# Quantizing the feed-forward weights inside the attention loop instead of ahead of it

## The chip, the cores and the metric

The kernel runs on one core of one Trainium2 chip. The time is the device time of one launch in microseconds (us). A core has five engines, each with an instruction queue of its own: TensorE (PE in the profile; PEld are its weight loads), VectorE (DVE), ScalarE (ACT), GpSimd (POOL) and SyncE (SP), which here only issues DMAs. They run side by side and wait for one another through semaphores. Sixteen DMA engines move the data; SP and ACT each issue into a queue of their own, and both queues are served by the same sixteen.

## The reference

```python
x = x + attention(layernorm(x), w_att_val, wv_w, wv_b, out_w, out_b)   # x: 16 x 512 x 256
x = x + ffn(layernorm(x), w_gate, w_up, w_down)                        # 256 -> 704 -> 256

# attention, 16 heads of 16 columns
att = softmax((x_h @ w_att[h]) @ x_h.T / sqrt(16));  o = att @ v_h;  return o @ out_w.T + out_b
# ffn
def fp4_quant_dequant(x):      # blocks of 16 along the last dim
    scale = max(max(abs(block)) / 6, 1e-12)
    return grid_round(abs(block / scale)) * sign * scale        # grid 0 .5 1 1.5 2 3 4 6
def fp4_linear(x, w): return fp4_quant_dequant(x) @ fp4_quant_dequant(w).T
return fp4_linear(silu(fp4_linear(x, w_gate)) * fp4_linear(x, w_up), w_down)
```

The three weight matrices of the feed-forward part are quantized once, before they are used. They do not depend on x. The change is about where this is done.

## The kernel before, in words

Three blocks follow one another, with a barrier of all engines between them.

`first_block` prepares batch 0 and the weights. It normalizes x, transposes it, makes the products q and the values v, and stores x and q, each split in a high and a low part, as rows in DRAM (`x_rows`, `q_rows`; `store`, L228). It also loads all three feed-forward matrices (L233 to L240), quantizes them in four chunks on DVE (`amax`, `scale_of`, `invert`, `in_units`, `shift`), ACT (`magnitude`) and POOL, transposes them on PE (`turn`), and stores them in DRAM (L253 to L256). The block ends when the last of these stores has landed.

`attention_block` runs over 16 batches b, in each over four quads g of four heads, and in each quad over four steps j; below, (g, j) names a step. Batches 1 to 13 run in a loop. While quad i is worked on, the row maxima of quad i+2 are made. In each step PE computes two maximum tiles (L858), the scores of four heads (L866, L869), two more maximum tiles, and then what else the step has: the product of probabilities and values (L885), or one or two of the small tasks that `IN_STEP` lists for the step. DVE reduces each of the four maximum tiles to one column (`reduce_max`, L1086), ACT makes the exponentials (L995), POOL splits and adds. All tiles of PSUM that are not scores share a ring of four banks, in the order of `TILES_IN_RING`. A tile may be written when the tile four places before it in the ring has been read. Two empty places (None) fill the ring's list up to 88.

The order on each engine is written out by hand, in the functions `quad` and `batch` of each engine. All waits stand in that order: an engine that waits for a semaphore holds back everything behind it.

SP's part of a batch, in order: for each quad g it stores half of the next batch's rows if g is even (`store_half`), waits until the scores of quad g are done, waits until the stores have landed (`stored`), and loads the stacks x_stack and q_stack of the next batch for this quad (`load_stacks`, L803 and L807, six DMAs).

ACT also issues DMAs: it stores the transposed maxima to DRAM (`store_maxima`, L1044), loads them as a stack (`load_maxima`, L1054), and loads x two batches ahead (L1058). PE's scores of a quad wait for the loaded maxima.

`ffn_block` then works through 64 tiles of 128 rows. It finds the weights in SBUF: SP loads them during the last batch.

Of the kernel before, what the change touches and what calls it, by code (L numbers as in the profile page):

```python
# [4 lines left out]
F32 = mybir.dt.float32  # L5
# [5 lines left out]
P = 128  # L11
B, T, E = 16, 512, 256
H, D = 16, 16
I = 704
# [11 lines left out]
STORES = (4 + 2) * 16  # L26
FK = [(k * P, min(P, I - k * P)) for k in range((I + P - 1) // P)]
# [41 lines left out]
def build(nc, x, w_att, wv_w, wv_b, out_w, out_b, w_gate, w_up, w_down, out):  # L69
# [8 lines left out]
    gate_up_kept = dram("gate_up_kept", [P, HALVES, 2 * I], F32)  # L78
    down_kept = dram("down_kept", [P, len(FK), E], F32)

    whole = ExitStack()
    with whole:
        def sb(name, shape, dt=F32, ctx=whole):
# [19 lines left out]
                 "stored0", "stored1")}  # L103

        with ExitStack() as prep:
            tiles = dict(
                qw_high=sb("qw_high", [P, HALVES, P], F32R, prep),
                qw_low=sb("qw_low", [P, HALVES, P], F32R, prep),
                vw_high=sb("vw_high", [P, HALVES, E], F32R, prep),
                vw_low=sb("vw_low", [P, HALVES, E], F32R, prep),  # L110
                v_bias=sb("v_bias", [P, E], F32, prep),
                xn=xn, splits=splits, v_dense=v_dense, stats=stats, mean_var=mean_var, rstd=rstd,
                minus_half=minus_half, eps=eps, ident=ident, x_all=x_all, out_T=out_T, out_bias=out_bias,
                x_rows=x_rows, q_rows=q_rows, gate_up_kept=gate_up_kept, down_kept=down_kept, sems=sems,
            )
            with ExitStack() as ctx:
                first_block(nc, ctx, x, w_att, wv_w, wv_b, out_w, out_b, w_gate, w_up, w_down, **tiles)
            with ExitStack() as ctx:
                attention_block(nc, ctx, x, max_rows, **tiles)
# [16 lines left out]
def first_block(nc, ctx, x, w_att, wv_w, wv_b, out_w, out_b, w_gate, w_up, w_down,  # L136
                xn, splits, v_dense, stats, mean_var, rstd, minus_half, eps, ident, x_all, out_T, out_bias,
                x_rows, q_rows, gate_up_kept, down_kept, sems, qw_high, qw_low, vw_high, vw_low, v_bias):
# [6 lines left out]
    def sem(name):  # L145
        return ctx.enter_context(nc.semaphore(name))

    NGU = 2 * I // P
    SPLIT, REST = I // P, I % P
    FULL = I // P  # L150
    gu = sb("gu", [P, NGU, E])
    gu_units = sb("gu_units", [P, NGU, E])
    gu_mag = sb("gu_mag", [P, NGU, E])
    dn = sb("dn", [P, HALVES, I])
    dn_units = sb("dn_units", [P, HALVES, I])
    dn_mag = sb("dn_mag", [P, HALVES, I])
    scale = sb("scale", [P, (NGU * E + HALVES * I) // BLK])
    inverse = sb("inverse", [P, (NGU * E + HALVES * I) // BLK])
    gate_up_T = sb("gate_up_T", [P, HALVES, 2 * I])
    down_T = sb("down_T", [P, len(FK), E])  # L160
# [15 lines left out]
    x_first, gu_loaded, dn_loaded, vw_loaded, ow_loaded, qw_loaded, bias_loaded, kept = (  # L176
        sem(n) for n in ("x_first", "gu_loaded", "dn_loaded", "vw_loaded", "ow_loaded", "qw_loaded",
                         "bias_loaded", "kept"))
# [6 lines left out]
    dn_quantized = sem("dn_quantized")  # L185

    amax_done, scale_done, inverse_done, units_done, mag_done, shifted, unshifted, quantized = (
        sem(n) for n in ("amax_done", "scale_done", "inverse_done", "units_done", "mag_done", "shifted",
                         "unshifted", "quantized"))


    def chunk(tiles, at, width, first):
        flat = [t[:, :, :].rearrange("p r e -> p (r e)")[:, at:at + width] for t in tiles]
        k = slice((first + at) // BLK, (first + at + width) // BLK)
        return (*flat, scale[:, k], inverse[:, k])

    GU_CHUNKS = [(r, min(4, NGU - r)) for r in range(0, NGU, 4)]
    CHUNKS = [chunk((gu, gu_units, gu_mag), r * E, n * E, 0) for r, n in GU_CHUNKS]
    CHUNKS.append(chunk((dn, dn_units, dn_mag), 0, HALVES * I, NGU * E))

# [4 lines left out]
    GATE_UP_FROM = len(TURNS)  # L207
    for c, (r, n) in enumerate(GU_CHUNKS):
        for a in range(HALVES):
            TURNS.append(([gu[:, k, a * P:(a + 1) * P] for k in range(r, r + n)],  # L210
                          gate_up_T[:, a, r * P:(r + n) * P], (quantized, c + 1)))
    for n in range(HALVES):
        TURNS.append(([dn[:, n, at:at + w] for at, w in FK[0:4]], down_T[:, 0:4, n * P:(n + 1) * P],
                      (dn_quantized, 1)))
    for k, (at, w) in enumerate(FK[4:]):
        TURNS.append(([dn[:, n, at:at + w] for n in range(HALVES)], down_T[0:w, 4 + k, :],
                      (dn_quantized, 1)))

    with nc.Block() as block:
        @block.sync  # L220
        def _(sp):
# [4 lines left out]
            def store(a, dst, rows):  # L226
# [4 lines left out]
            load_x(0, 2, x_first)  # L231
            sp.dma_start(vw[:, :, :], wv_w.rearrange("(n p) e -> p n e", p=P)).then_inc(vw_loaded, 16)
            sp.dma_start(gu[:, 0:SPLIT, :], w_gate[0:SPLIT * P, :].rearrange("(r p) e -> p r e", p=P))\  # L233
              .then_inc(gu_loaded, 16)
            sp.dma_start(gu[0:REST, SPLIT, :], w_gate[SPLIT * P:I, :]).then_inc(gu_loaded, 16)
            sp.dma_start(gu[REST:P, SPLIT, :], w_up[0:P - REST, :]).then_inc(gu_loaded, 16)
            sp.dma_start(gu[:, SPLIT + 1:NGU, :], w_up[P - REST:I, :].rearrange("(r p) e -> p r e", p=P))\
              .then_inc(gu_loaded, 16)
            sp.dma_start(v_bias[:, :], wv_b.partition_broadcast(P)).then_inc(bias_loaded, 16)
            sp.dma_start(dn[:, :, :], w_down.rearrange("(n p) k -> p n k", p=P)).then_inc(dn_loaded, 16)  # L240
# [9 lines left out]
            for c, (r, n) in enumerate(GU_CHUNKS):  # L250
                sp.wait_ge(moved, GATE_UP_FROM + HALVES * (c + 1))
                cols = slice(r * P, (r + n) * P)
                sp.dma_start(gate_up_kept[:, :, cols], gate_up_T[:, :, cols]).then_inc(kept, 16)  # L253
            sp.wait_ge(moved, len(TURNS))
            sp.dma_start(down_kept[:, 0:FULL, :], down_T[:, 0:FULL, :]).then_inc(kept, 16)
            sp.dma_start(down_kept[0:I - FULL * P, FULL, :], down_T[0:I - FULL * P, FULL, :]).then_inc(kept, 16)  # L256
            sp.wait_ge(bias_loaded, 32)
            for a in range(HALVES):
                sp.wait_ge(stored[a], STORES)
            sp.wait_ge(kept, 16 * (len(GU_CHUNKS) + 2))  # L260

        @block.gpsimd
        def _(pool):
# [20 lines left out]
            for c, (src, units, mag, sc, inv) in enumerate(CHUNKS[:-1]):  # L284

                pool.wait_ge(unshifted, c + 1)
                pool.tensor_tensor(blocks(src), blocks(units), spread(sc, BLK), ALU.mult).then_inc(quantized, 1)

        @block.scalar
        def _(act):  # L290
# [12 lines left out]
            def magnitude(c):  # L303
                act.wait_ge(units_done, c + 1)
                act.activation(CHUNKS[c][2], CHUNKS[c][1], ACT.Abs, scale=2.0 ** 22).then_inc(mag_done, 1)


# [8 lines left out]
            magnitude(0)  # L316
# [3 lines left out]
            magnitude(1)  # L320
            move(1)
            magnitude(2)
            for n in range(2, 2 + HALVES):
                move(n)
            magnitude(3)
            for n in range(2 + HALVES, len(TURNS)):
                move(n)
# [1151 lines left out]
```

## Time and profile before

| | us |
|---|---|
| median of 3 runs | 1574.35 (1573.51 to 1575.29) |
| the profiled execution | 1576.56 |
| its span | 1574.5 |
| `first_block` and its barrier end | 55.0 |
| first scores of batch 0 | 86.0 |
| `ffn_block` begins, about | 1003 |

Rows of the page and of the trace read as follows. A timeline row is start, duration of the whole group, engine, line, operation, destination and sources, shapes and number of instructions; in brackets stands how long the engine was idle before, and what ended this. A row of windows gives the stretch, its length, then the busy time and the instructions of PE, PEld, DVE, ACT and POOL, TensorE's granted clock as a share of full speed, the busy share of the DMA engines and the GB/s. SPq and ACTq are DMAs issued by SP and ACT; their duration is the time that issuing takes.

### The profile page before, as it was taken

Reading aid. Unit: us, or ns where it says so; the run is one execution under the profiler, and the core shown is the slowest. Engines: PE = TensorE matmul, PEld = TensorE weight load, DVE = VectorE, ACT = ScalarE, POOL = GpSimd, SP = SyncE. Lnnn points to the kernel's source line nnn. Section 1 sums busy time; section 2 is a strip of 40 time slices with the busy share of each in tenths; the row PEclk is TensorE's granted clock in tenths of the full one; section 3 lists DMA queues with packets and bytes.
Section 4 is the critical chain, followed back from the end, with each engine's and each line's share of the span. In section 5 each row is a group of like instructions: output and inputs, shape, how many; then the busy total and the mean of one; then the engine's idle time right before and its main releaser. Section 6 shows DMA issues by size and latency. Waiting matters only on the chain. (4 is left out here: it accounts for less than half of the span.)

```text
span 1574.5 us, 33229 instructions
## 1 busy us (share of the span) xinstructions
PE 1460.8 (93%) x8874; PEld 910.1 (58%) x8874; DVE 1313.4 (83%) x2603; ACT 864.9 (55%) x1778; POOL 634.1 (40%) x868
## 2 busy tenths in 40 slices
PE   3389999999999999999999998699999999999998
PEld 3145555555555555555555554466666666676665
DVE  7588887888888888788788774499999999999995
ACT  2157777677677677777767767233333333333332
POOL 2135445345345444544544521133434334343341
PEclk8589999999999999999999999799999999999999
DMA  5534564555554455455455460000000000000000
GB/s 195 149 111 136 140 160 124 148 149 133 138 159 124 127 160 148 122 136 162 122 142 156 112 163 29 1 10 14 17 17 13 17 13 17 17 13 17 13 17 20
DMA packets 81762, 144.07 MB, mean 91 GB/s; under 512 B 19904, under 2 KB 39488, under 8 KB 81600
## 3 DMA queue, kind: packets, MB, share of 16 engines
q1 hardware_dynamic: 64992, 134.19, 30.7%
q10 hardware_dynamic: 16736, 9.46, 2.7%
q8 instruction: 17, 0.28, 0.1%
q14 instruction: 17, 0.14, 0.0%
HBM read 81.67 MB, written 61.93 MB: 91 GB/s over the span
## 5 line engine op out<-in xcount | busy, mean ns | idle before, releaser
L1086 DVE TENSOR_REDUCE neg_max<-ring 128x1 f32<-128x512 f32 x1024 | 636.7, 683 | 137.6 <-PE ring L858 136.5
L995 ACT ACTIVATE probs<-scores 128x512 f32<-128x512 f32 x1024 | 528.9, 605 | 211.6 <-PE scores L869 206.0
L1411 PE MATMUL gu_bank<-splits,f_x_T 128*128 128x352 f32 x1024 | 317.3, 463 | 2.1 <-ACT f_x_T L1389 2.1
L858 PE MATMUL ring<-x_stack,q_stack 64*128 64x512 f32 x1024 | 234.5, 455 | 45.5 <-DVE neg_max L1086 16.8
L1411 PEld LDWEIGHTS gu_bank<-splits,f_x_T 128*128 128x128 f32 x1024 | 191.5, 192 | 99.3 <-issue 3.0
L885 PE MATMUL ring<-probs,v_quad 128*32 128x512 f32 x2048 | 246.2, 598 | 1.9
L858 PEld LDWEIGHTS ring<-x_stack,q_stack 64*128 64x128 f32 x1024 | 99.1, 188 | 196.2 <-DVE neg_max L1086 132.6
L866 PE MATMUL scores<-q_stack,x_stack 64*128 64x512 f32 x1024 | 206.0, 396 | 2.1 <-ACT probs L995 2.1
L869 PE MATMUL scores<-max_stack,max_ones 64*128 64x512 f32 x1024 | 203.8, 392 | 0.0
L1239 POOL TENSOR_TENSOR f_rstd<-f_mean_var,eps 128x1 f32<-128x1 f32 x64 | 44.7, 699 | 330.9 <-DVE f_mean_var L1349 330.9
L733 POOL TENSOR_TENSOR pv_rows<-pv_more,pv_rows 128x512 f32<-128x512 f32 x64 | 82.2, 1285 | 199.7 <-ACT pv_more L1001 194.9
L1369 ACT ACTIVATE h_T<-h_bank 128x512 f32<-128x512 f32 (+1 forms) x128 | 49.0, 435 | 195.0 <-PE h_bank L1421 195.0
L1429 PE MATMUL y_bank<-splits,h_T 128*128 128x256 f32 x640 | 150.4, 382 | 1.1 <-ACT h_T L1369 1.1
L885 PEld LDWEIGHTS ring<-probs,v_quad 128*32 128x32 f32 x2048 | 53.6, 109 | 126.3 <-issue 74.2
L1429 PEld LDWEIGHTS y_bank<-splits,h_T 128*128 128x128 f32 x640 | 117.5, 192 | 15.4 <-issue 0.8
L710 POOL TENSOR_TENSOR max_cols<-neg_max,one 128x16 fp32r<-128x16 f32 x64 | 13.8, 216 | 244.2 <-DVE neg_max L1086 244.2
L869 PEld LDWEIGHTS scores<-max_stack,max_ones 64*128 64x128 f32 x1024 | 98.1, 185 | 20.0
L866 PEld LDWEIGHTS scores<-q_stack,x_stack 64*128 64x128 f32 x1024 | 98.2, 186 | 19.9 <-ACT probs L995 8.3
L1249 POOL TENSOR_TENSOR hq<-h_level,h_scale 128x704 f32<-128x704 f32 x64 | 88.5, 1383 | 25.2 <-DVE h_level L1294 25.2
L1306 DVE TENSOR_SCALAR f_xn<-x_all,f_mean_var,f_rstd 128x256 f32 (+1 forms) x64 | 83.2, 1300 | 10.0 <-POOL f_rstd L1242 5.8
L1389 ACT ACTIVATE f_x_T<-x_bank 128x256 f32<-128x256 f32 x64 | 24.6, 384 | 119.3 <-PE x_bank L1399 119.3
L1381 ACT ACTIVATE gate<-gu_bank 128x352 f32<-128x352 f32 x128 | 58.7, 458 | 40.1 <-PE gu_bank L1411 40.0
(130 smaller groups left out, 2076.8 us busy)
## 6 DMA issues: line engine op xcount, KB each, us to landing
x_rows<-splits SPq DMA_DIRECT2D x128, 256.0 KB, 2.8
x_stack<-x_rows SPq DMA_DIRECT2D x128, 256.0 KB, 4.3
q_stack<-q_rows SPq DMA_DIRECT2D x256, 128.0 KB, 4.3
q_rows<-splits SPq DMA_DIRECT2D x64, 256.0 KB, 2.2
out_dram<-x_all SPq DMA_DIRECT2D x64, 128.0 KB, 1.7
x_all<-in_L_attn_x_dram ACTq DMA_DIRECT2D x14, 512.0 KB, 6.4
max_stack<-max_rows ACTq DMA_DIRECT2D x128, 8.0 KB
splits<-gate_up_kept SPq DMA_DIRECT2D x1, 1408.0 KB, 7.5
```

What stands on the lines that cost most here:

```text
L733: pool.tensor_tensor(pv_rows[g % 2][:, :], pv_more[:, :], pv_rows[g % 2][:, :], ALU.add)\
L858: pe.matmul(bank(tiles[m])[:, :], row_tile(q_stack[q], m)[:, p, s * P:(s + 1) * P], row_tile(x_stack[q], m)[:, p, :], start=True, stop=Tru ...
L866: pe.matmul(scores[ROWS * p + m][:, :], row_tile(x_stack[g], m)[:, p, j * P:(j + 1) * P], row_tile(q_stack[g], m)[:, p, :], start=True, st ...
L869: pe.matmul(scores[ROWS * p + m][:, :], row_tile(max_ones, m)[:, 0, :], row_tile(max_stack[g % 2], m)[:, p, :], start=False, stop=True).th ...
L885: m = pe.matmul(bank(tile)[VW * h:VW * h + VW, :], v[q][:, j, h, :], probs[j][:, k, :], start=(j == steps[0]), stop=(j == steps[1]))
L995: act.activation(probs[j][:, k, :], scores[k][:, :], ACT.Exp).then_inc(p_ready, 1)
L1086: dve.tensor_reduce(neg_max[g % 2][:, at:at + 1], tile[:, :], AX.X, ALU.max, negate=True).then_inc(m_used, 1)
L1249: pool.tensor_tensor(blocks(out), blocks(level), spread(scale, BLK), ALU.mult).then_inc(done, 1)
L1306: dve.tensor_scalar(xn[w][:, :], x_all[:, bass.ds(m, 1), :].rearrange("p o e -> p (o e)"), mean_var[w][:, 0:1], rstd[w][:, :], ALU.subtrac ...
L1381: act.activation(gate[1 - u][:, k, :], gu_bank[k][:, :], ACT.Silu).then_inc(gate_done, 1)
L1411: m = pe.matmul(gu_bank[c][:, :], x_T[u][:, a, :], gate_up_T[:, a, c * CH:(c + 1) * CH], start=(a == 0), stop=(a == HALVES - 1))
L1429: m = pe.matmul(y_bank[:, :], h_T[u][0:width, k, :], down_T[k][0:width, :], start=(k == 0), stop=(k == len(FK) - 1))
```

## The change

Nothing of the feed-forward weights is left in `first_block`. It loads x of batch 0 alone first and x of batch 1 a little later, and at its end SP loads the stacks of quads 0 and 1 of batch 0.

At the start of `attention_block` ACT issues twelve DMAs (`copy_weights`) that copy the three matrices from DRAM to DRAM into 42 slabs of 128x128 (64 KB each). Each of batches 0 to 13 takes three slabs. SP loads them into `w_raw` (`load_weights`), DVE, POOL and ACT quantize them in steps (1, 0) to (2, 2), and in step (1, 1) of the following batch PE turns them, ACT copies them to `w_turned` and SP stores them (`store_weights`). Two more things change in the steps: the ring gets the tile "weights" in (1, 1) and one empty place fewer, and in (3, 3) "proj1" now comes before "rows2". POOL's two instructions "tie" and "units" take the place of DVE's one instruction `in_units`.

```diff
-    IN_STEP = {... (1, 1): ("rows0",), ... (3, 3): ("rows2", "proj1")}
+    IN_STEP = {... (1, 1): ("weights", "rows0"), ... (3, 3): ("proj1", "rows2")}
+    WEIGHTS = {(1, 0): "peak", (1, 1): "scale", (1, 2): "invert", (2, 0): "shift", (2, 1): "unshift"}
     POOL_STEP = {...
-                 (2, 1): ("halves",), (2, 2): ("deviation",), ...
+                 (1, 2): ("tie", "units"), ...
+                 (2, 1): ("halves",), (2, 2): ("deviation", "quantized"), ...
# SP, batch(b), in each quad g
                         sp.wait_ge(s_ready, QUAD * TT * (i + 1))
-                        load_stacks(b + 1, g)
+                        load_stacks(sp, b + 1, g, x_stack, q_stack, x_rows, q_rows, stored, stack_loaded)
+                        if g == 0 and quantizing(b):
+                            load_weights(b)
+                        if g == 1 and stands("weights", b):
+                            store_weights(b)
+            def load_weights(b):
+                if isinstance(b, int) and b == 0:
+                    sp.wait_ge(w_copied, 16 * COPIES)
+                else:
+                    sp.wait_ge(w_quantized, b)
+                sp.dma_start(w_raw[:, :].rearrange("p (s c) -> p s c", c=P),
+                             slabs[bass.ds(UNIT * b, UNIT)].rearrange("s p c -> p s c")).then_inc(w_loaded, 16)
+            def store_weights(b):
+                sp.wait_ge(kept_used, use("weights", b, BY_ACT) + 1)
+                sp.dma_start(slabs_kept[...], w_turned[...]).then_inc(w_stored, 16)
# DVE, weights(task, b), called after the third reduce_max of its step
+                if task == "peak":
+                    dve.wait_ge(w_loaded, 16 * (b + 1))
+                    dve.tensor_reduce(w_scale[:, :], blocks(w_raw[:, :]), AX.X, ALU.max, apply_absolute_value=True)\
+                       .then_inc(w_peak, 1)
+                elif task == "scale": ...     # tensor_scalar, 128x24
+                elif task in ("shift", "unshift"): ...   # scalar_tensor_tensor, 128x384
+                else: ...                     # reciprocal, 128x24
# ACT: 128x384, after (1, 3) and in (1, 1); PE in (1, 1)
+                act.activation(w_level[:, :], w_units[:, :], ACT.Abs, scale=2.0 ** 22).then_inc(w_magnified, 1)
+                act.activation(w_turned[:, :], bank("weights")[:, 0:UNIT * P], ACT.Copy).then_inc(kept_used, 1)
+                for s in range(UNIT):
+                    m = pe.transpose(out[:, s * P:(s + 1) * P], w_level[:, s * P:(s + 1) * P], ident[:, :])
# ACT, ahead of store_maxima(0, 0)
+            copy_weights()
```

How the instructions stand. First SP, in batch 0 from the stores of q_rows on (x_stack and q_stack are the stacks of the next batch, quad 0 and then quad 1). Before:

```order
L814 DMA q_rows<-splits 128x512 [waits q_low]
L814 DMA q_rows<-splits 128x512
L803 DMA x_stack<-x_rows 64x1024 [waits stored0,s_ready]
L807 DMA q_stack<-q_rows 32x1024 x2
L803 DMA x_stack<-x_rows 64x1024
L807 DMA q_stack<-q_rows 32x1024 x2
L803 DMA x_stack<-x_rows 64x1024 [waits stored0,s_ready]
```

and now:

```order
L723 DMA q_rows<-splits 128x512 [waits q_low]
L723 DMA q_rows<-splits 128x512
L154 DMA x_stack<-x_rows 64x1024 [waits stored0,s_ready]
L158 DMA q_stack<-q_rows 32x1024 x2
L154 DMA x_stack<-x_rows 64x1024
L158 DMA q_stack<-q_rows 32x1024 x2
L749 DMA w_raw<-slabs 128x3x128 [waits w_copied]
L154 DMA x_stack<-x_rows 64x1024 [waits stored0,s_ready]
```

The load of w_raw stands behind the six loads of quad 0's stacks, which themselves wait for the stores of q_rows to land.

Next DVE, in batch 0 from the last maxima of quad 0 to those of step (1, 1). w_scale is the blocks' scale of the three slabs. The rows of before:

```order
L1086 TENSOR_REDUCE neg_max<-ring 128x1 [waits m_ready] x16
L1095 STREAM_TRANSPOSE max_turned<-max_cols 128x32 [waits max_stored,m_low]
L1101 BN_STATS stats<-x_all 128x6 [waits x_loaded,mv_done]
L1086 TENSOR_REDUCE neg_max<-ring 128x1 [waits m_ready] x4
L1124 RECIPROCAL recip<-ring 128x16 [waits misc_ready]
L1127 TENSOR_TENSOR o_rows<-ring,recip 128x4x64 [waits recip_done]
```

Now:

```order
L1074 TENSOR_REDUCE neg_max<-ring 128x1 [waits m_ready] x15
L1102 TENSOR_REDUCE w_scale<-w_raw 128x24 [waits w_loaded]
L1074 TENSOR_REDUCE neg_max<-ring 128x1 [waits m_ready]
L1083 STREAM_TRANSPOSE max_turned<-max_cols 128x32 [waits max_stored,m_low]
L1089 BN_STATS stats<-x_all 128x6 [waits x_loaded,mv_done]
L1074 TENSOR_REDUCE neg_max<-ring 128x1 [waits m_ready] x3
L1106 TENSOR_SCALAR w_scale<-w_scale 128x24 [waits w_peak]
L1074 TENSOR_REDUCE neg_max<-ring 128x1 [waits m_ready]
```

The reduction of w_raw, which waits for the load, has come between the third and the fourth maximum of step (1, 0). Behind it stand the fourth maximum, the transposed maxima and everything else of DVE.

Last PE, at the end of a batch, in step (3, 3) and the first tiles of step (0, 0) (ident and pv_rows are rows2's transposes, out_T and o_T the projection). Before:

```order
L866 MATMUL scores<-q_stack,x_stack 128x512 x2
L869 MATMUL scores<-max_stack,max_ones 128x512 x2
L858 MATMUL ring<-x_stack,q_stack 128x512 x2
L922 MATMUL ring<-ident,pv_rows 128x128 x4
L937 MATMUL ring<-out_T,o_T 128x256 x4
L858 MATMUL ring<-x_stack,q_stack 128x512 x2
```

and now:

```order
L798 MATMUL scores<-q_stack,x_stack 128x512 x2
L801 MATMUL scores<-max_stack,max_ones 128x512 x2
L790 MATMUL ring<-x_stack,q_stack 128x512 x2
L869 MATMUL ring<-out_T,o_T 128x256 x4
L854 MATMUL ring<-ident,pv_rows 128x128 x4
L790 MATMUL ring<-x_stack,q_stack 128x512 x2
```

The projection has moved ahead of the transposes.

## Rows read from the trace of the kernel before

**Rows 1.** The page, part 1: busy time, share of the span, instructions.
```profile
PE 1460.8 (93%) x8874; PEld 910.1 (58%) x8874; DVE 1313.4 (83%) x2603; ACT 864.9 (55%) x1778; POOL 634.1 (40%) x868
```

**Rows 2.** Windows, one batch of the loop; columns as told above.
```profile
251.00:308.00 57.00, 54.96 (x410) 31.83 (x410) 46.56 (x89) 40.52 (x78) 26.95 (x38) 1.00 0.53 140
```

**Rows 3.** Timeline, steps (1, 0) to (1, 2) of one batch, DVE and PE.
```profile
212.34 2.48 DVE L1086 TENSOR_REDUCE neg_max<-ring 128x1 f32<-128x512 f32 x4 [1.18 <-PE ring L858]
...
214.87 0.39 DVE L1101 BATCH_NORM_STATS2 stats<-x_all 128x6 f32 x1
...
215.81 2.48 DVE L1086 TENSOR_REDUCE neg_max<-ring 128x1 f32<-128x512 f32 x4 [0.56 <-PE ring L858]
...
216.54 0.39 PE L858 MATMUL ring<-x_stack,q_stack 64*128 64x512 f32 x2
...
217.58 0.63 PE L922 MATMUL ring<-ident,pv_rows 128*128 128x128 f32 x4 [0.65 <-POOL pv_rows L733]
...
218.14 0.49 PE L858 MATMUL ring<-x_stack,q_stack 64*128 64x512 f32 x2
...
219.22 2.46 DVE L1086 TENSOR_REDUCE neg_max<-ring 128x1 f32<-128x512 f32 x4
```

**Rows 4.** Timeline of SP, the same batch: DMAs issued.
```profile
214.34 0.85 SPq L814 DMA_DIRECT2D q_rows<-splits  x2
217.07 0.52 SPq L803 DMA_DIRECT2D x_stack<-x_rows  x1
...
219.53 0.92 SPq L807 DMA_DIRECT2D q_stack<-q_rows  x2
```

**Rows 5.** Loads of x_stack, 195 to 500 us: from issue to landing.
```profile
DMA to landing us min/median/max: 3.6/4.3/6.9
```

**Rows 6.** Page, DMA issues: operation, count, KB each, median us to landing.
```profile
out_dram<-x_all SPq DMA_DIRECT2D x64, 128.0 KB, 1.7
```

**Rows 7.** Windows of 1 us behind the loads of rows 4.
```profile
222.00:223.00 1.00, 1.00 (x10) 0.82 (x10) 0.69 (x3) 0.74 (x2) 0.00 (x0) 1.00 0.92 205
223.00:224.00 1.00, 1.00 (x9) 0.63 (x8) 1.00 (x3) 1.00 (x3) 0.00 (x0) 1.00 0.22 45
```

**Rows 8.** DVE's groups by shape, 0 to 60 us: busy us, mean ns.
```profile
L414 DVE SCALAR_TENSOR_TENSOR gu_units<-gu_mag,gu_units 128x1024 f32<-128x1024 f32 x4 | 4.8, 1217 | 0.0
...
L391 DVE TENSOR_REDUCE scale<-gu 128x48 f32<-128x768 f32 x1 | 1.0, 968 | 0.0
```

**Rows 9.** Windows: TensorE's clock where PE stops, and where it resumes.
```profile
24.00:26.00 2.00, 1.13 (x10) 0.93 (x8) 2.00 (x5) 1.50 (x2) 0.00 (x0) 1.00 1.03 383
26.00:28.00 2.00, 0.00 (x0) 0.00 (x0) 2.00 (x3) 0.05 (x1) 0.00 (x0) 1.00 0.19 70
28.00:30.00 2.00, 0.00 (x0) 0.00 (x0) 2.00 (x6) 0.00 (x0) 0.00 (x0) 0.61 0.01 4
...
93.00:94.00 1.00, 0.67 (x7) 0.53 (x8) 0.41 (x2) 0.60 (x1) 0.23 (x1) 0.86 0.00 0
```

**Rows 10.** Timeline, step (2, 1): DVE's last maximum, PE behind it.
```profile
231.97 0.66 DVE L1086 TENSOR_REDUCE neg_max<-ring 128x1 f32<-128x512 f32 x1
...
232.69 0.19 PEld L858 LDWEIGHTS ring<-x_stack,q_stack 64*128 64x128 f32 x2 [0.36 <-DVE neg_max L1086]
```

**Rows 11.** Timeline, from step (3, 3) to (0, 0).
```profile
252.34 1.89 PE L937 MATMUL ring<-out_T,o_T 128*128 128x256 f32 x8
...
255.14 0.50 PE L858 MATMUL ring<-x_stack,q_stack 64*128 64x512 f32 x2 [0.91 <-DVE x_all L1136]
```

**Rows 12.** Timeline, the first block and the start of the second.
```profile
14.16 1.20 DVE L391 TENSOR_REDUCE scale<-gu 128x64 f32<-128x1024 f32 x1
...
22.77 1.80 SPq L228 DMA_DIRECT2D q_rows<-splits  x4
...
55.01 0.52 SPq L803 DMA_DIRECT2D x_stack<-x_rows  x1
...
62.64 1.22 PE L858 MATMUL ring<-x_stack,q_stack 64*128 64x512 f32 x4 [11.78 <-DMA q_stack<-q_rows]
...
75.80 1.14 ACTq L1044 DMA_DIRECT2D max_rows<-max_turned  x1
...
85.96 0.66 PE L866 MATMUL scores<-q_stack,x_stack 64*128 64x512 f32 x2
```

More of the change, by code:

```diff
@@ L102, in build @@
                 ("bn_done", "mv_done", "rstd_base", "rstd_done", "xn_done", "xh_done", "qh_done",
-                 "stored0", "stored1")}
+                 "stored0", "stored1", *(f"stack_loaded{g}" for g in range(QUADS)))}
         with ExitStack() as prep:
@@ L248, in _ @@
                 store(a, q_rows, (qh, ql))
[L250 to L256, printed above, removed]
             sp.wait_ge(bias_loaded, 32)
-            for a in range(HALVES):
-                sp.wait_ge(stored[a], STORES)
-            sp.wait_ge(kept, 16 * (len(GU_CHUNKS) + 2))
+            for g in range(2):
+                load_stacks(sp, 0, g, x_stack, q_stack, x_rows, q_rows, stored, stack_loaded)
         @block.gpsimd
@@ L365, in _ @@
                     m.then_inc(v_made, 1)
-            for n in range(2, len(TURNS)):
-                turn(n)
         @block.vector
@@ L587, in stands @@
             return False
-        return {0: kind not in FINISH, B - 1: kind not in PREPARE,
+        return {0: kind not in FINISH and kind != "weights", B - 1: kind not in PREPARE and kind != "weights",
                 B: kind in FINISH}.get(b, True)
@@ L597, in use @@
         else:
-            before = len(kinds) * b - sum(k in FINISH for k in kinds)
+            before = len(kinds) * b - sum(not stands(k, 0) for k in kinds)
         return before + order.index(kind)
@@ L604, in uses_before @@
             return sum(stands(k, n) for n in range(b) for k in kinds)
-        return len(kinds) * b - sum(k in FINISH for k in kinds)
+        return len(kinds) * b - sum(not stands(k, 0) for k in kinds)
     def in_ring(tile, b):
@@ L1035, in quad @@
                             keep(kind, b + 1)
+                        if stands(kind, b) and kind == "weights":
+                            keep_weights(b)
+                    if (g, j) == (1, 3) and quantizing(b):
+                        weight_magnitude(b)
                     if j == 0 and not (last and g == 3):
@@ L1157, in quad @@
                             reduce_max(i + 2, (g + 2) % QUADS, TT * j + s)
+                        if s == 2 and quantizing(b) and (g, j) in WEIGHTS:
+                            weights(WEIGHTS[g, j], b)
                         if j == 0 and s == 3 and turning:
```

306 lines of the change are left out of this document (147 added, 159 removed).

## The prediction, made before the changed kernel had run

> **What bounds the kernel now.** I read the page first. PE is busy for 93% of the span and DVE for 83% [rows 1]; in one batch of the loop, 57.0 us long, PE is busy for 54.96 us and DVE for 46.56 us, with the clock at full speed (2.4 GHz) [rows 2]. So the loop is bound by PE's order, with DVE close behind. Then I read the timeline step by step, since it shows how tightly the two are coupled. DVE starts four maxima at 212.34 and again at 215.81, each time as soon as PE has written the next tiles, having been idle for 1.18 and 0.56 us [rows 3]. PE for its part may write a tile only when the one four places before it in the ring has been read. An engine that is held for long therefore stops the other within half a step. Third I read SP's queue, because the change puts a DMA into it, and a DVE instruction waits for this DMA. Fourth the first 86 us, where the other part of the change lies.
>
> **The load that comes too late.** This is the largest term. In each of batches 0 to 13 DVE's "peak" in step (1, 0) waits for the load of w_raw which SP issues in quad 0 of the same batch. SP issues it behind the loads of the next batch's stacks. Those begin at 217.07, when the stores of q_rows, issued from 214.34, have landed; the last of them is issued from 219.53 to 220.45 [rows 4]. One issue is preceded by some 0.15 us of register work, so w_raw goes out at 220.6. DVE comes to "peak" after three of the four maxima that start at 212.34 and take 2.48 us, 0.62 each: at 214.2 [rows 3]. The load would have to be there 6.4 us before it is issued.
>
> When does it land? The stacks' data is still being moved in the stretch 222 to 223 (DMA share 0.92, 205 GB/s) and nearly gone in the next (0.22) [rows 7], so w_raw's 0.19 MB begin at about 223.2 and need 0.9 us at that rate. With 0.2 us for the semaphore that is 224.3, 3.7 us after issue. Bounds: 1.7 us after issue, as the output's stores of 128 KB take [rows 6], and 6.9 us, the longest of the stack loads, whose shortest is 3.6 and median 4.3 [rows 5]. That is 222.3 to 227.5. I take 224.3, near the 3.6 of a stack load that queues behind few others.
>
> DVE then does "peak", 128x384. The reduction of 128x768 took 0.968 us [rows 8], so this one about 0.5. The fourth maximum ends at 224.3 + 0.5 + 0.65 = 225.45. The transpose (0.2) and the statistics (0.39) [rows 3] bring it to 226.05, where before it was at 215.26. The four maxima of (1, 1) and "scale" (0.12) end at 226.05 + 2.48 + 0.12 = 228.65.
>
> PE has by then stopped. Its second pair of (1, 1), at 216.54 before, needs the fourth maximum of (1, 0): it comes at 225.5. The three turns of the weights (a transpose of 128x128 starts about 0.15 us after the one before: 0.45 us) fit into what was an idle 0.65 us ahead of rows0 [rows 3], since the POOL result is long there. But the new tile shifts the ring: the first pair of (1, 2) now needs the fourth maximum of (1, 1), where before it needed the third. It comes at 228.7 instead of 218.14, 10.55 us late, and DVE's next maxima, at 219.22 before, come at 229.75, as late. ACT is held as well: it stores the maxima of the transpose behind the fourth maximum before it makes the exponentials of (1, 1). It makes them from 225.8 to 227.9, which is still ahead of PE at 228.7. So a batch loses 10.55 us here; by the bounds of the landing 8.55 to 13.75.
>
> Could something give it back? The wait is counted from the stores of q_rows, thus from the batch's own quad 0, and comes again in each batch. In the loop nothing is idle for that long. SP's later loads have more time than before, which is worth nothing.
>
> **The clock.** PE has nothing to do from about 216.9 to 225.5, some 8.6 us. In the first block PE's last work ends at 25.1 and the granted clock falls inside the stretch 28 to 30 (0.61 on average, full until 28.4 if it is half after that), 3.3 us later [rows 9]. So it will fall to 1.2 GHz in each stall. The other way, PE worked densely from 85.96 on, and the clock rose in the stretch 93 to 94 (0.86, so at 93.3) [rows 9, 12], 7.3 us later. PE resumes at 225.5 and would then be at full clock at about 232 to 233. Until 228.7 DVE is the limit and the slow clock costs nothing; from there to 232.3 PE is the limit and does half as much as it could: 1.8 us per batch. Bounds 0 (it does not fall, or rises by 228.7) and 4 us.
>
> The Trainium skill's page "TensorE: Matmul & The Clock Gate", section "HAM oscillation — how this bites in real kernels", says that a wait for a DMA in each pass of a loop, if it is long enough, throttles the array anew in each pass, and that the cost is half the throttled time. It speaks against this change, and the first block's row agrees with its first half; no row here shows it inside a loop.
>
> **The other work in the loop.** "Shift" and "unshift" are 128x384 each; 128x1024 took 1.217 us [rows 8], so about 0.5 each. "Shift" in (2, 0) is covered by DVE's idle half microsecond there. "Unshift" in (2, 1) is not: DVE works without a gap up to 232.63, and PE's next pair starts right behind it at 232.69, having waited for it for 0.36 us [rows 10]. I take 0.6 us per batch with its semaphore, bounds 0 and 1.0. "Invert" (about 0.3) lies in DVE's gap in (1, 2). ACT's two instructions of 128x384 (0.5 each) fall where ACT waits for PE. POOL gets three of about 0.9 us and was busy for 26.95 of 57.0 us [rows 2]; "units" waits long for "invert", but behind it stand only the next quad's maxima, which come later. The extra loads and stores (0.4 MB per batch) meet a DMA share of 0.53 [rows 2].
>
> The new order in (3, 3) gains. Before, the projection ran from 252.34 to 254.23, DVE then added it for 0.69 us, and PE waited 0.91 us for this to 255.14 [rows 11]. Now the projection starts half a microsecond sooner, the addition lies beside the transposes, and one empty place is gone from the ring. 0.45 us gained at 14 ends of batches (1 to 14): 6.3 us, bounds 0 and 12.6.
>
> **The head.** Before, the stacks of batch 0 were first loaded at 55.01, PE began the maxima at 62.64 and the scores at 85.96 [rows 12]. Now SP loads the first stacks once q_rows has landed. Its stores began at 22.77 [rows 12]; on DVE some 5 us of weight work between 14.16 and that time fall away, and x of batch 0 comes alone and so sooner. Stores at about 17.5 to 19.5, landed by 21, twelve loads of 0.52 us to 27.5, barrier, PE's first maxima at 29. From there to the scores it took 85.96 - 62.64 = 23.3 us, DVE's 34 maxima: 52.3. But ACT's twelve copies, 2.75 MB, now stand ahead of the first maxima's store in ACT's queue, and share the engines with 3 MB of stacks. That store was issued 10.2 us ahead of the scores [rows 12] and needs some 4 us with its load, so 6 us of delay are free. No row shows a copy from DRAM to DRAM: at the 383 GB/s of [rows 9] it is 7 us, at 205 GB/s [rows 7] with the bytes counted twice 27 us. Between, with the stacks, I take the scores at 57.5: a gain of 28.5 us, bounds 20 and 34.
>
> **The sum.** Against the profiled execution, 1576.56: 14 x (10.55 + 1.8 + 0.6) = 181.3; less 6.3; less 28.5: +146.5, so 1723.1. The profiled execution was 2.2 us above the median of the runs, so I forecast 1721.
>
> The Trainium skill's page "DMA: Bandwidth & Descriptors", section "Anatomy of one DMA — SWDGE (gpsimd) path", gives a fixed cost of about 2.0 us and the bytes at 436 GB/s for a DMA (measured on another issuing path). By it w_raw would land 2.45 us after issue, at 223.05, and the sum would be 14 x 1.25 = 17.5 us lower, about 1703. The trace's shortest 3.6 us [rows 5] speaks against it here.
>
> **Rivals.**
> - The clock is not lost, or only where DVE is the limit: 14 x 1.8 = 25 us less, 1696. For it: PE does some work between 225.5 and 228.7. Against: a gap far over the 3.3 us of [rows 9]. Chance 0.22.
> - It is worse: w_raw lands at 225.5 and the clock stays low to 235, 14 x 2.7 = 38 us more, 1759; or the copies take all of the head's gain. Chance 0.20.
> - The faster side: w_raw is there when DVE comes to "peak". Then a batch costs only 0.6 and about 0.4 for the shifted ring, and the sum is 1574.35 + 14 - 6.3 - 28.5 = 1553.5. It decides at 214.2 in the batch: the load would have to be issued by 211, ahead of the stores of q_rows at 214.34 [rows 4]. SP's order forbids that, unless I misread which batch's load "peak" waits for. Chance 0.04.
> - Part of the wait is hidden and the head's gain pays the rest, within 0.2% of before: this needs the wait to shrink to 2 us per batch. Chance 0.01.
> - The forecast itself: 0.53.
>
> A change of less than about 0.2% (3 us) can't be told from none. Faster 0.04, same 0.01, slower 0.95. Taking the bounds of landing (-28, +45), clock (-25, +31), unshift, batch end and head together, not all at one end, the range is 1672 to 1780.
>
> **What would show it.** In the profile after, DVE's idle time before the reduction of w_raw is about 10 us, 14 times, ended by the DMA w_raw<-slabs; SP issues this DMA right behind the stacks; a batch of 0 to 13 takes about 69.5 us instead of 57.0, the later ones 57; the clock shows dips in each batch; the first scores stand at 55 to 60. If DVE has no idle time there, I am wrong altogether. If batches take 67.7 us, the clock term is wrong; if the first scores come after 65, the copies are.

## The result and the profile after

The changed kernel took 1713.97 us (median of 4 runs, 1710.9 to 1716.49) against 1574.15 for the kernel before in the same session (1573.51 to 1575.29). The ratio is 1.088, with a 95% interval of 1.0862 to 1.0898. The forecast was 1721, slower. The profiled execution took 1710.9 us, with a span of 1709.1.

Part 1 of the page, and one batch of the loop as a row of windows, answer to [rows 1, 2]:

```profile
PE 1488.8 (87%) x8882; PEld 924.0 (54%) x8882; DVE 1312.7 (77%) x2648; ACT 866.9 (51%) x1792; POOL 662.2 (39%) x909
```

```profile
243.00:312.00 69.00, 57.59 (x413) 33.70 (x413) 48.50 (x95) 41.75 (x82) 29.35 (x41) 0.93 0.46 123
```

DVE has 45 instructions more over the whole kernel and is busy for as long as before. What grew is the time in which nothing is done: a batch takes 69 us instead of 57, and the clock's mean in it is 0.93 instead of 1.00. The page's row of the new reduction names the cause (line, engine, operation, tiles, shapes, count; busy us and mean ns; idle time before, and its releaser):

```profile
L1102 DVE TENSOR_REDUCE w_scale<-w_raw 128x24 f32<-128x384 f32 x14 | 7.7, 553 | 153.6 <-DMA w_raw<-slabs 153.6
```

DVE waited 153.6 us in 14 batches, 10.97 us each. The timeline of one batch, SP, DVE and PE, answers to [rows 3, 4]:

```profile
206.43 0.85 SPq L723 DMA_DIRECT2D q_rows<-splits  x2
...
208.30 0.39 PE L801 MATMUL scores<-max_stack,max_ones 64*128 64x512 f32 x2
...
211.60 0.91 SPq L158 DMA_DIRECT2D q_stack<-q_rows  x2
212.70 0.40 SPq L749 DMA_DIRECT2D w_raw<-slabs  x1
217.11 0.55 DVE L1102 TENSOR_REDUCE w_scale<-w_raw 128x24 f32<-128x384 f32 x1 [10.86 <-DMA w_raw<-slabs]
...
218.32 0.80 PE L790 MATMUL ring<-x_stack,q_stack 64*128 64x512 f32 x2 [9.63 <-DVE neg_max L1074]
...
220.39 0.17 DVE L1106 TENSOR_SCALAR w_scale<-w_scale 128x24 f32<-128x24 f32 x1
...
221.21 0.80 PE L790 MATMUL ring<-x_stack,q_stack 64*128 64x512 f32 x2
...
225.88 0.50 PE L790 MATMUL ring<-x_stack,q_stack 64*128 64x512 f32 x2
```

SP issues the load right behind the last stack. DVE has by then been waiting since 206.25 (217.11 - 10.86), and PE stops at 208.7. The last line but one is the first pair of (1, 2), where the loss of the stall can be read: step (1, 0) began at 203.83 here and at 211.84 before, and this pair stands 11.08 us further from it than it did. The last line is the first pair of (1, 3). It comes 4.67 us later; in the kernel before, the same pair came 3.66 us after the one at 218.14 of [rows 3]:

```profile
221.80 0.50 PE L858 MATMUL ring<-x_stack,q_stack 64*128 64x512 f32 x2
```

Over all 14 loads the view of this line gives the landing:

```profile
DMA to landing us min/median/max: 4.1/4.4/5.0
```

Windows of 1 us show the clock in the same stall; they answer to [rows 9]:

```profile
213.00:214.00 1.00, 0.00 (x0) 0.00 (x0) 0.00 (x0) 0.00 (x0) 0.00 (x0) 0.83 1.04 225
214.00:215.00 1.00, 0.00 (x0) 0.00 (x0) 0.00 (x0) 0.00 (x0) 0.00 (x0) 0.50 1.04 216
...
223.00:224.00 1.00, 1.00 (x6) 0.33 (x2) 0.36 (x1) 1.00 (x3) 0.00 (x0) 0.55 0.00 0
224.00:225.00 1.00, 1.00 (x14) 0.38 (x16) 0.88 (x3) 0.95 (x2) 0.00 (x0) 1.00 0.00 0
```

The clock falls to 1.2 GHz at 213.7, 5.0 us after PE stopped, and is back at 2.4 GHz at 223.9, 5.6 us after PE resumed. The DMA share of 1.04 in the stall is the traffic of the stacks and of w_raw itself.

The timeline at the end of a batch answers to [rows 11], and the start of the kernel to [rows 12]:

```profile
256.42 1.99 PE L869 MATMUL ring<-out_T,o_T 128*128 128x256 f32 x8
258.25 0.60 PE L854 MATMUL ring<-ident,pv_rows 128*128 128x128 f32 x4
259.33 0.50 PE L790 MATMUL ring<-x_stack,q_stack 64*128 64x512 f32 x2 [0.47 <-DVE x_all L1142]
```

```profile
20.33 0.57 SPq L154 DMA_DIRECT2D x_stack<-x_rows  x1
...
28.13 1.22 PE L790 MATMUL ring<-x_stack,q_stack 64*128 64x512 f32 x4 [7.43 <-DMA q_stack<-q_rows]
...
29.36 5.60 ACTq L1035 DMA_DIRECT2D slabs<-in_L_ffn_w_up_dram  x1
...
45.99 1.12 ACTq L1001 DMA_DIRECT2D max_rows<-max_turned  x1
...
52.65 0.66 PE L798 MATMUL scores<-q_stack,x_stack 64*128 64x512 f32 x2
```

PE's wait for the residual shrank from 0.91 to 0.47 us. The first scores come at 52.65 instead of 85.96, a gain of 33.3 us.

Where the time is, between the two profiled executions: the load of x two batches ahead, which opens each batch, is a good mark. Its register move is issued in batches 1 to 13. The first line is the kernel before, the second the changed one (minimum, median and maximum duration, then the first and last start):

```profile
L1058 ACTq MOVE x_all<-in_L_attn_x_dram x13: 29/29/29, 139.3 to 822.3; - x13
```

```profile
L1015 ACTq MOVE x_all<-in_L_attn_x_dram x13: 29/29/29, 118.4 to 946.9; - x13
```

A batch took (822.3 - 139.3) / 12 = 56.92 us and takes 69.04. Head -33.3; batch 0 from its first scores to the mark of batch 1, 65.7 instead of 53.3: +12.4; twelve batches +145.5; from the last mark to the end of the span +10.0. Sum +134.6, the difference of the spans.

The three matrices fill only 34 of the 42 slabs, which the description of the change does not say. The last eight are copies of parts of w_gate that the feed-forward block never reads (`filler` in `copy_weights`), and batches 12 and 13 work on nothing else (slabs 36 to 41). Two of the 14 waits are therefore paid for no result, by an estimate from the two periods some 2 x 12 = 24 us. Leaving them out wasn't tried.

### The profile page after: what moved, and what is told of

It reads as the page before. It is cut to its first block and busy times, and to the rows that moved or that the text cites. A ratio compares the mean times of both kernels' runs of the same rounds, so it can differ in the third digit from the quotient of the medians.

```text
span 1709.1 us, 33554 instructions
## 1 busy us (share of the span) xinstructions
PE 1488.8 (87%) x8882; PEld 924.0 (54%) x8882; DVE 1312.7 (77%) x2648; ACT 866.9 (51%) x1792; POOL 662.2 (39%) x909
## 5 line engine op out<-in xcount | busy, mean ns | idle before, releaser
L790 PE MATMUL ring<-x_stack,q_stack 64*128 64x512 f32 x1024 | 245.2, 477 | 179.7 <-DVE neg_max L1074 163.0
L798 PE MATMUL scores<-q_stack,x_stack 64*128 64x512 f32 x1024 | 210.8, 406 | 2.0 <-ACT probs L937 2.0
L801 PE MATMUL scores<-max_stack,max_ones 64*128 64x512 f32 x1024 | 207.9, 401 | 0.0
L1102 DVE TENSOR_REDUCE w_scale<-w_raw 128x24 f32<-128x384 f32 x14 | 7.7, 553 | 153.6 <-DMA w_raw<-slabs 153.6
L798 PEld LDWEIGHTS scores<-q_stack,x_stack 64*128 64x128 f32 x1024 | 101.9, 194 | 20.4 <-ACT probs L937 7.9
```

The costliest lines, as they stand in the source:

```text
L790: pe.matmul(bank(tiles[m])[:, :], row_tile(q_stack[q], m)[:, p, s * P:(s + 1) * P], row_tile(x_stack[q], m)[:, p, :], start=True, stop=Tru ...
L798: pe.matmul(scores[ROWS * p + m][:, :], row_tile(x_stack[g], m)[:, p, j * P:(j + 1) * P], row_tile(q_stack[g], m)[:, p, :], start=True, st ...
L801: pe.matmul(scores[ROWS * p + m][:, :], row_tile(max_ones, m)[:, 0, :], row_tile(max_stack[g % 2], m)[:, p, :], start=False, stop=True).th ...
```

## The experiments

Each ratio below is against the kernel before on the same chip, with its 95% interval. "Period" is the batch's length between the marks just described.

**The load moved to the start of SP's batch.**

```diff
                 for g in range(QUADS):
                     if not last:
+                        if g == 0 and quantizing(b):
+                            load_weights(b)
                         if g % 2 == 0:
                             store_half(b + 1, g // 2)
                         ...
                         load_stacks(...)
-                        if g == 0 and quantizing(b):
-                            load_weights(b)
```

> The load of w_raw for batch b is issued at the start of SP's part of batch b, ahead of the stores of x_rows and q_rows, some 10 us before DVE's reduction wants it; nothing else differs from the changed kernel. My theory (the late load, and the clock that falls in its wait, are the whole loop term): DVE's idle time ahead of the reduction of w_raw goes from 153.6 us in 14 waits to nearly nothing, the clock stays at full speed in the loop, a batch takes 57.0 + 0.36 (shifted ring) + 0.46 (unshift) - 0.35 (end of batch) = 57.5 us, and the time is 1574 - 33.3 + 14 x 0.47 = about 1547 us. Rival (the added instructions on DVE and POOL themselves stretch the steps, and the wait only shows where the time collects): batches stay above 62 us and the time above 1620 us.

Measured: 1556.22 us, ratio 0.988 (0.9865 to 0.9895). The period is 57.87 us. The groups by line list no wait for w_raw, and the clock is full over the loop; the rival, with batches above 62 us, is excluded:

```profile
L1015 ACTq MOVE x_all<-in_L_attn_x_dram x13: 29/29/29, 105.7 to 800.1; - x13
```

```profile
200.00:500.00 300.00, 287.19 (x2126) 166.88 (x2128) 252.76 (x485) 214.11 (x414) 152.69 (x214) 1.00 0.54 144
```

So the place of one DMA in SP's order is worth some 158 us, and with it the sign of the whole change. The faster-side rival of the prediction said 1553.5 for this case. The kernel is still some 9 us slower than this experiment's expectation. Batches of 57.87 instead of 57.5 make 5 of these; the profiled run was 4 us below the median, and the last experiment's part below comes back to that spread.

**The load issued behind the stores of q_rows, ahead of the wait for them.**

```diff
                         if g % 2 == 0:
                             store_half(b + 1, g // 2)
+                        if g == 0 and quantizing(b):
+                            load_weights(b)
                         sp.wait_ge(s_ready, QUAD * TT * (i + 1))
                         load_stacks(...)
-                        if g == 0 and quantizing(b):
-                            load_weights(b)
```

> The load of w_raw is issued right behind the stores of q_rows and ahead of the wait for the scores and of the stack loads, about 5.4 us sooner than in the changed kernel. It should land about 3 us after issue, and DVE's wait shrink from 10.9 to about 4 us, so PE is idle for about 2.8 us instead of 9.6. My theory of the clock (it falls only after more than 3.3 us without PE work): full speed through the whole loop, a batch takes 69.06 - 6.9 (wait) - 1.0 (clock) = 61.2 us, time about 1714 - 14 x 7.9 = 1604 us. Rival (the clock costs nothing here, the loss is the wait alone): the clock rows may or may not dip, and the time is 1714 - 14 x 6.9 = 1617 us.

Measured: 1612.18 us, ratio 1.024 (1.0217 to 1.0263). DVE waits 3.79 us per batch and the period is 61.89 us. The wait came out as expected, the clock did not, and the time lies between the expectation's two cases (1604 and 1617). PE's timeline and windows:

```profile
195.53 0.40 PE L801 MATMUL scores<-max_stack,max_ones 64*128 64x512 f32 x2
198.57 0.50 PE L790 MATMUL ring<-x_stack,q_stack 64*128 64x512 f32 x2 [2.64 <-DVE neg_max L1074]
199.58 0.55 PE L878 MATMUL ring<-ident,w_level 128*128 128x128 f32 x3 [0.52 <-DVE neg_max L1074]
```

```profile
200.00:201.00 1.00, 0.78 (x6) 0.42 (x4) 1.00 (x4) 1.00 (x4) 0.00 (x0) 0.93 1.03 240
201.00:202.00 1.00, 0.54 (x2) 0.50 (x4) 0.97 (x4) 0.93 (x3) 0.00 (x0) 0.50 0.98 235
...
207.00:208.00 1.00, 1.00 (x10) 0.19 (x4) 0.00 (x0) 0.04 (x1) 0.00 (x0) 0.66 0.00 0
```

PE was idle for 2.64 us, and the clock fell at 200.9, when PE was at work again, and in this batch stayed low until 207.7. My reading of [rows 9], that the clock falls 3.3 us after PE has stopped and therefore needs a gap of that length, does not hold.

**The load issued between the stores of x_rows and those of q_rows**, to shorten the gap further.

```diff
             def store_half(b, c, a):
                 store(c, a, x_rows, f"x{a}", (xh, xl, xl, xh))
+                if a == 0 and quantizing(b):
+                    sp.wait_ge(q_low, HALVES * (c - 1) + a + 1)
+                    load_weights(b)
                 store(c, a, q_rows, f"q{a}", (qh, ql))
```

> The changed kernel with the load of w_raw issued just ahead of the two stores of q_rows (behind those of x_rows), about 1 us sooner than in the version with the load behind q_rows. There DVE waited 3.8 us, PE stood idle for 2.64 us, and the clock fell 5.0 us after PE had stopped, 2.3 us after PE had taken up a thin stretch of work; it came back 5.6 us after the work was dense. Here DVE should wait 2.8 us and PE stand idle for about 1.6 us. If the idle stretch itself decides, the clock now stays full and a batch takes 61.94 - 1.0 - 2.9 = 58.0 to 58.5 us, 1563 us in all. If the thin stretch around the stall is enough, the clock falls again and a batch takes about 61 us, 1599 us.

Measured: 1605.95 us, ratio 1.0199 (1.0181 to 1.0218), period 61.46 us. The groups by line give DVE's wait (us, times), and PE's timeline and the windows the rest:

```profile
  DMA w_raw<-slabs: 38.6, 14
```

```profile
197.43 0.68 PE L791 MATMUL ring<-x_stack,q_stack 64*128 64x512 f32 x2 [1.64 <-DVE neg_max L1075]
```

```profile
197.00:198.00 1.00, 0.57 (x2) 0.19 (x2) 1.00 (x4) 0.00 (x0) 0.92 (x2) 0.79 0.03 10
198.00:199.00 1.00, 0.67 (x5) 0.50 (x3) 1.00 (x3) 0.65 (x2) 1.00 (x2) 0.50 0.25 29
...
204.00:205.00 1.00, 1.00 (x12) 0.32 (x8) 1.00 (x3) 0.45 (x1) 0.67 (x1) 0.79 0.08 21
```

The stall with a gap of 1.64 us was enough: the clock fell at 197.6 and came back at 204.4. The expectation's second case holds. Compared with the experiment before, the wait shrank by 1.03 us per batch and the period by only 0.43. In the early-load kernel, where PE waits 0.91 us at (1, 2), the clock stays full. So a wait can cost more than its length once the clock falls with it. The period grew by 61.46 - 57.87 = 3.59 us for a wait of 2.76 us, although one instruction of DVE, "scale", became 0.5 us faster in it (more on this below).

The price of the clock can be read within this run. Of two batches that follow one another, from mark to mark, the clock fell in the first and not in the second:

```profile
605.25:666.66 61.41, 57.33 (x412) 32.82 (x411) 48.38 (x94) 41.44 (x81) 29.32 (x41) 0.97 0.51 137
666.66:726.51 59.85, 55.77 (x412) 32.27 (x411) 48.27 (x94) 41.39 (x81) 29.30 (x41) 1.00 0.52 140
```

The fall cost 1.56 us. PE's gap was 1.46 us in the first of them and 1.51 us in the second, so the length of the gap does not tell in which batch the clock falls. What does is not shown here.

**No weight work in the loop.** The feed-forward weights are neither quantized nor turned; the ring keeps an empty place where "weights" was, the copies remain.

```diff
         def quantizing(b):
-            return not isinstance(b, int) or b < UNITS
+            return False
-    IN_STEP = {... (1, 1): ("weights", "rows0"), ...
+    IN_STEP = {... (1, 1): ("rows0",), ...
+                if (g, j) == (1, 1):
+                    TILES_IN_RING.append(None)
```

> All work on the weights inside the loop is left out (no load of w_raw, no quantization, no turning, no storing), and the feed-forward block gets the copied weights as they are, neither quantized nor turned; the ring keeps an empty place where the weights' tile was, and the copies and the first block stay as in the changed kernel. It shows the head's gain and the new end of the batch alone. My theory: 1574.2 - 33.3 - 14 x 0.35 = 1536 us, with batches of 56.65 us. Rival (part of the head's gain is given back later, by transfers or at the change of blocks): above 1542 us.

Measured: 1539.21 us, ratio 0.9761 (0.9747 to 0.9774):

```profile
L1014 ACTq MOVE x_all<-in_L_attn_x_dram x13: 29/29/29, 107.3 to 785.2; - x13
```

The period is (785.2 - 107.3) / 12 = 56.49 us. Its loop differs from the loop before in the order of (3, 3), the place of one empty tile, and in `recip`, which now has two buffers, and it is 0.43 us shorter per batch. I take that as the end-of-batch term; the order alone, in the kernel before, wasn't tried. The time lies between the expectation (1536) and its rival (above 1542), so that this run does not tell them apart.

**"Unshift" one step later**, on top of the early load.

```diff
-    WEIGHTS = {... (2, 0): "shift", (2, 1): "unshift"}
+    WEIGHTS = {... (2, 0): "shift", (2, 2): "unshift"}
-                 (2, 2): ("deviation", "quantized"), (2, 3): ("q1",), ...
+                 (2, 2): ("deviation",), (2, 3): ("q1", "quantized"), ...
```

> As e1_load_early, and in addition unshift is moved from step (2, 1) to (2, 2), where PE does not wait for DVE's last maximum, and POOL's last instruction behind q1 in (2, 3). My theory (unshift in (2, 1) costs 0.46 us of PE per batch): 14 x 0.46 = 6 us below e1, about 1541 us. Rival (PE waits in (2, 2) or later instead, or q1's split was the cover): the same as e1 within 2 us.

Measured: 1552.86 us, ratio 0.9844 (0.9829 to 0.9859). The period is 57.34 us, 0.53 less. "Unshift" in (2, 1) did cost what it takes. The medians differ by only 3.4 us instead of the expected 6, which is inside the spread of the runs; the period carries this verdict. The level of 1541 was again too low, and the timeline of this kernel shows by what:

```profile
188.35 1.04 POOL L647 TENSOR_TENSOR splits<-raw_x,one 128x512 fp32r<-128x512 f32 x1
...
188.56 0.87 DVE L1106 TENSOR_SCALAR w_scale<-w_scale 128x24 f32<-128x24 f32 x1
...
190.07 0.50 PE L790 MATMUL ring<-x_stack,q_stack 64*128 64x512 f32 x2 [0.91 <-DVE neg_max L1074]
```

"Scale", a 128x24 instruction, takes 0.87 us here and took 0.17 in the changed kernel. It ends at 189.43, when POOL's instruction does (189.39). In the changed kernel POOL's work stood elsewhere after the stall.

**"Scale" moved to where POOL is idle**, on top of the version before.

```diff
-    WEIGHTS = {(1, 0): "peak", (1, 1): "scale", (1, 2): "invert", ...
+    WEIGHTS = {(1, 0): "peak", (1, 2): "invert", ...
                             turn_maxima(i + 1, (g + 1) % QUADS, first and g == 0)
+                        if (g, j, s) == (1, 0, 3) and quantizing(b):
+                            weights("scale", b)
```

> The version with the early load and unshift in (2, 2), and 'scale' now directly behind the transposed maxima of step (1, 0) instead of behind the third maximum of (1, 1). In the two early-load kernels the 128x24 tensor_scalar took 0.85 us and ended within 0.05 us of POOL's 128x512 splits beside it; in the changed kernel, with POOL idle there, the same instruction took 0.17 us. Theory (it stands still while POOL's elementwise work runs): at the new place POOL is idle, it takes 0.17 us, the fourth maximum of (1, 1) comes 0.85 us sooner, PE's wait of 0.91 us ahead of (1, 2) shrinks to about 0.1, and a batch of 1 to 13 takes 57.3 - 0.6 = 56.7 us: about 1545 us. Rival (it takes 0.85 us since it waits for its own input w_peak, or the ring sets PE's wait anyway): no shorter batch, 1553.

Measured: 1541.76 us, ratio 0.9778 (0.9763 to 0.9793). The groups by line of "scale", of the version before and of this one, and this one's marks:

```profile
L1106 DVE TENSOR_SCALAR w_scale<-w_scale x14: 850/856/867, 75.4 to 819.2; 128x24 f32<-128x24 f32 x14
```

```profile
L1106 DVE TENSOR_SCALAR w_scale<-w_scale x14: 133/134/136, 73.0 to 808.7; 128x24 f32<-128x24 f32 x14
...
L1015 ACTq MOVE x_all<-in_L_attn_x_dram x13: 29/29/29, 108.4 to 788.8; - x13
```

The period is 56.70 us, 0.64 less, as expected. The rival is excluded: the batch did get shorter, and the instruction's own input cannot have held it, since it now follows its input more closely. The Trainium skill's page "SBUF — State Buffer", section "Who interferes with whom", says that a tensor_scalar can enter a mode in which it needs the port pair that DVE shares with GpSimd, and that it then waits for the whole GpSimd instruction that holds the pair; the two groups agree. Against the loop without any weight work this is 0.21 us per batch: with three placements changed the quantization is almost free, and the kernel is 2.2% faster than the one before.

**Ten of the twelve copies issued later**, on top of this.

```diff
-            copy_weights()
+            copy_weights(True)
             store_maxima(0, 0)
             load_maxima(0, 0)
+            copy_weights(False)
```

The two copies that batch 0 needs come first and have a semaphore of their own; SP waits for the other ten from batch 1 on.

> The same, and in addition only the two copies that batch 0 needs stand ahead of the first store of maxima in ACT's queue; the other ten are issued behind the load of these maxima. Theory (the head is held by ten of the copies, which share the DMA engines with the stacks and block ACT's queue until 45.9): the store of the maxima is issued at about 41.5 instead of 46.0, the first scores come at about 51 instead of 52.5, and the kernel gains 1 to 2 us on the version before it: 1544. Danger: the ten copies now hold ACT's queue for some 10 to 18 us while the first exponentials stand behind them; if that is later than the scores of step (0, 0), PE stops in batch 0 and up to 10 us are lost.

Measured: 1541.85 us, ratio 0.9778 (0.9759 to 0.9797). No gain. ACT's issues and PE's first scores:

```profile
41.12 1.12 ACTq L1005 DMA_DIRECT2D max_rows<-max_turned  x1
...
43.81 1.31 ACTq L1041 DMA_DIRECT2D slabs<-in_L_ffn_w_up_dram  x2
...
52.46 0.66 PE L802 MATMUL scores<-q_stack,x_stack 64*128 64x512 f32 x2
```

The store of the maxima goes out 4.9 us sooner than in the changed kernel (45.99), and the first scores come 0.2 us sooner (0.5 sooner than in the version before it). So the copies blocked ACT's queue, and nothing waited for it. The danger named in the expectation didn't come either, since behind the stacks' loads an issue takes 0.65 us instead of up to 5.6 in the changed kernel and 8.3 in the version before this one.

**The spread of the head.** Two windows show why runs of one kernel differ by some 4 us. The first fence is the version with "scale" moved, the second the one with split copies; their first scores are at 52.98 and 52.46:

```profile
56.00:58.00 2.00, 1.90 (x10) 1.53 (x12) 1.83 (x5) 0.35 (x2) 0.00 (x0) 0.50 0.00 0
64.00:66.00 2.00, 2.00 (x18) 0.46 (x12) 0.66 (x2) 0.15 (x1) 1.23 (x3) 0.79 0.98 366
```

```profile
54.00:56.00 2.00, 1.25 (x8) 0.48 (x8) 1.17 (x2) 1.62 (x4) 0.00 (x0) 0.66 0.52 177
56.00:58.00 2.00, 1.83 (x16) 1.10 (x12) 2.00 (x6) 1.07 (x3) 0.00 (x0) 1.00 0.05 8
```

In the one TensorE's clock rises at about 64.8, in the other at 55.4. Batch 0 then reaches the mark of batch 1 at 108.4 and at 104.7. The medians are equal, so this is chance in the run rather than the copies' doing. The early load and the version with "unshift" later, whose heads are alike, show the same: there the clock rises at 55.0 and at 65.0, and the mark of batch 1 stands at 105.7 and at 109.2. I infer it from these four traces; it wasn't tried by itself.

## Why the prediction was right, and where it was off

**The late load: right.** Issue behind the stacks, DVE's wait, PE's stall and its place came as worked out. The landing took 4.4 us (median) after issue instead of 3.7. DVE waited 10.97 us instead of 10.1, and the first pair of (1, 2) came 11.08 us late instead of 10.55. The 0.2 us for the semaphore in the sum of the landing are seen in no run by themselves; the runs show the landing as a whole. In the first-listed experiment the wait and all of its loss went with the place of the load.

**The clock: right in that it fell, too large, and for a reason that does not hold.** I took 1.8 us per batch. From (1, 2) to (1, 3) PE lost another 1.0 us (4.67 against 3.66): the clock was back at 223.9, and only from 221.2 on was PE the limit. The steps "falls 3.3 us after" and "rises 7.3 us after" were 5.0 and 5.6 here; the fall came after 4.9 us with the gap of 2.64 us and after 1.8 with that of 1.64 us. With them falls my argument against the first rival, that a gap has to be longer than 3.3 us. A rough cross-check, from the periods: 69.04 - 57.87 - 10.97 + 0.69 (scale no longer held) = 0.9 us; with the gaps of 2.64 and 1.64 us it is 0.9 and 1.4. In the second of these the pair of batches above gives 1.56 us directly. The term also differs from batch to batch: in four of the changed kernel's twelve batches from mark to mark the mean clock is 0.90, and they took 69.8 us on average; in the other eight it is 0.93, and they took 68.7. The Trainium skill's page "TensorE: Matmul & The Clock Gate", section "HAM oscillation — how this bites in real kernels", says that a DMA wait in every pass, if long enough, throttles the array anew in every pass: the trace agrees. It makes the length of the gap the condition; in the runs with 2.64 and 1.64 us of idle time the clock fell all the same, which the section does not lead one to expect, and there the measurement decides.

**The other work.** "Unshift": 0.6 us taken, 0.46 read in the changed kernel's timeline at (2, 2), 0.53 by the experiment. "Scale": 0.12 taken, 0.17 measured; but the faster-side rival counted it at the same price, and there it takes 0.85. The end of a batch: 0.45 taken, 0.35 in the timeline (from (2, 2) to the next batch), 0.43 by the experiment.

**The head: the mis-sized term.** I took a gain of 28.5 us and it was 33.3, near the upper bound of 34. The first maxima were right (29 taken, 28.13 measured). The step that failed is the copies: I let them delay the first scores from 52.3 to 57.5. They blocked ACT's queue, in one issue for 5.60 us, and made the store of the maxima 4.9 us late. That is inside the 6 us which I had called free and then did not use. The experiment with ten copies later moved the scores by 0.2 us.

**The sum.** 14 x (11.08 + 1.0 + 0.46) - 14 x 0.35 - 33.3 = +137.4, where the profiled executions differ by 134.3 and the forecast said +146.5. Of the 9.1 us between the two sums the clock makes 11.2, the head 4.8 and "unshift" 2.0, while the wait (7.4) and the end of the batch (1.4) went the other way. That the total came close owes something to these two signs, and so to luck. One price among the rivals was added up wrongly: landing at 225.5 and a low clock to 235 make 1.2 + (235 - 229.9) / 2 - 1.8 = 1.95 us per batch and not 2.7, thus 1748 and not 1759. It changes neither the forecast nor the verdict.

## What to carry to other kernels

When work is spread into a tuned loop, look first at the queue that brings its data: write down when the consumer reaches its first instruction and when the DMA is issued behind everything ahead of it in that queue. Here the computing cost 0.2 us per batch and the DMA's place 11. A wait in an engine's fixed order can also cost TensorE its clock, and then the last microseconds of it are the dear ones: cutting DVE's wait from 10.97 to 3.79 us took 7.15 us off the batch, cutting it to 2.76 took another 0.43, and taking these last 2.76 us away took 3.59. Check also that the work in the loop is work that somebody needs in each pass. Then place small DVE instructions by what POOL does beside them, not only by what DVE has free.

## What was not expected of the hardware

- The clock fell in a loop with a PE gap of only 1.64 us, 1.8 us after PE had stopped, and stayed low for 6.8 us (197.6 to 204.4). With a gap of 2.64 us it was also low for 6.8 us (200.9 to 207.7), with one of 9.6 us for 10.2 us (213.7 to 223.9). With gaps of 0.9 us it stayed full. The first two are early batches of their runs; in most later ones the mean clock over a batch was 0.97, about half as long at 1.2 GHz, and in one, with a gap of 1.51 us, it did not fall.
- A 128x24 tensor_scalar took 0.13 and 0.17 us with POOL idle, and 0.85 us when it ended together with POOL's 128x512 instruction.
- Copies from DRAM to DRAM, issued beside and just behind SP's stack loads, held ACT for 5.60 us at one issue, 3.85 at another and 3.56 at two together, while three before them took 0.64 to 0.77 each. Issued once the stack loads were over, they took about 0.65 us each, although the DMA share was 1.07 there (46 to 52 us in the run with split copies).
- The same load of w_raw, 192 KB, landed 2.6 us after issue (median) when issued ahead of the stacks, and 4.4 us behind them. In the early load, where it stands behind the last stacks of the batch before, it took 5.9 us, and nothing waited for it.
